# Rows loaded and normed a stage ahead, inverse roots on GpSimd, projections as paired row tiles

## What is computed

```python
h = tok(x)                                  # q,k,v; (gamma * (q k^T)) v; Wo; prelu
h = concatenate([h, txt], axis=1)           # 8 x 1056 x 64
h = h + L0_attn(layernorm(h), ...)          # 8 heads of 8, softmax(q k^T + bias[i-j]) v, proj + bias
h = h + L0_ffn(layernorm(h), ...)           # top 2 of 16 experts 64->128->64, then a layernorm
h = h + L1_attn(layernorm(h), ...)          # linear attention: elu+1, q (k^T v), Wproj + bias
h = h + L1_ffn(layernorm(h), ...)           # rmsnorm, 4 heads with rope, causal softmax, wo; rmsnorm, top 2 of 8 experts (silu)
```

## Time and profile before

| | |
|---|---|
| median of three runs | 2918.41 us (2917.83 to 2937.95) |
| profiled execution, its own time | 2931.52 us |
| its span | 2929.7 us |
| busy: PE, DVE, ACT, POOL | 88%, 68%, 53%, 12% |
| mean granted PE clock | 0.887 |

### The profile page before, as it was taken

One profiled execution on the slowest core, in us unless ns is written; L12 is line 12 of the kernel. 1 busy time (PEld: TensorE's weight loads), 2 busy tenths in 40 slices (PEclk: granted clock), 3 DMA queues, 4 the chain that ended last, 5 costly groups with the idle time before them and its releaser, 6 DMA issues. The chain is left out here.

```text
span 2929.7 us, 52672 instructions
## 1 busy us (share of the span) xinstructions
PE 2564.9 (88%) x18552; PEld 1160.8 (40%) x18552; DVE 1987.7 (68%) x5083; ACT 1552.4 (53%) x2645; POOL 354.0 (12%) x456
## 2 busy tenths in 40 slices
PE   5987659999999999997699997986679998789999
PEld 3323542333333333335333333564544444623333
DVE  5686668888888888871477775737667774256665
ACT  2332654777777777772244443615646666134443
POOL 1020100000000000003112211011101011221110
PEclk9998767999999999996699997755589999589999
DMA  2101991112212212213300001233422231511100
GB/s 72 22 15 27 279 281 51 48 45 55 56 38 56 55 38 55 70 17 85 67 17 17 22 16 24 61 85 124 160 104 72 66 91 35 123 28 29 29 15 20
DMA packets 308491, 188.23 MB, mean 64 GB/s; under 512 B 262069, under 2 KB 263414, under 8 KB 306982
## 3 DMA queue, kind: packets, MB, share of 16 engines
q1 hardware_dynamic: 297870, 165.80, 21.4%
q0 software_dynamic: 10368, 19.06, 2.1%
HBM read 103.16 MB, written 81.69 MB: 63 GB/s over the span
## 5 line engine op out<-in xcount | busy, mean ns | idle before, releaser
L1614 DVE TENSOR_REDUCE att_mpart<-ps 128x1 f32<-128x512 f32 x1024 | 637.3, 684 | 81.2 <-PE ps L1423 48.5
L1571 ACT ACTIVATE att_p<-ps 128x704 f32<-128x704 f32 x768 | 543.3, 760 | 139.5 <-PE ps L1487 134.5
L1516 PE MATMUL ps<-att_p,att_v 128*32 128x352 f32 x3072 | 308.4, 472 | 0.1
L1423 PE MATMUL ps<-att_kT,att_qT 64*128 64x512 bf16 x1024 | 274.5, 387 | 27.5 <-DMA att_qz<-qt_d 14.2
L1487 PE MATMUL ps<-att_qm,att_kT 64*128 64x352 bf16 x1536 | 251.1, 317 | 10.8 <-ACT att_p L1571 8.0
L1243 DVE TENSOR_REDUCE cau_mpart<-ps 128x1 f32<-128x512 f32 (+5 forms) x384 | 193.5, 552 | 90.8 <-PE ps L1069 70.7
L2285 ACT ACTIVATE mo_act<-ps,mo_b 128x768 f32<-128x768 f32 x176 | 156.3, 901 | 129.5 <-PE ps L2167 129.5
L2478 DVE TENSOR_TENSOR mo_g<-mo_act,ps 128x768 f32<-128x768 f32 x176 | 167.4, 951 | 79.5 <-PE ps L2202 43.5
L1210 ACT ACTIVATE cau_p<-ps 128x704 f32<-128x704 f32 (+6 forms) x272 | 171.6, 660 | 82.5 <-PE ps L1128 49.7
L2865 ACT ACTIVATE mo_act<-ps 128x1024 f32<-128x1024 f32 (+1 forms) x108 | 102.9, 953 | 196.3 <-PE ps L2779 196.0
L1487 PEld LDWEIGHTS ps<-att_qm,att_kT 64*128 64x128 bf16 x1536 | 82.4, 93 | 279.8 <-issue 263.6
(11 more groups left out here) (432 smaller groups left out, 4367.2 us busy)
## 6 DMA issues: line engine op xcount, KB each, us to landing
v_d<-pre_v SPq DMA_DIRECT2D x32, 288.0 KB, 4.3
qs_d<-pre_qs SPq DMA_DIRECT2D x8, 1152.0 KB, 5.6
att_qs<-qs_d SPq DMA_DIRECT2D x32, 288.0 KB, 4.5
att_v<-v_d SPq DMA_DIRECT2D x32, 288.0 KB, 4.4
qt_d<-pre_qT SPq DMA_DIRECT2D x8, 1056.0 KB, 4.4
kt_d<-pre_kT SPq DMA_DIRECT2D x8, 1056.0 KB, 7.6
att_kT<-kt_d SPq DMA_DIRECT2D x32, 264.0 KB, 2.7
att_qT<-qt_d SPq DMA_DIRECT2D x32, 264.0 KB, 3.1
```

Of the source, the lines that this page charges most:

```text
L1423: mm = pe.matmul(ps[:, bank, :], qT[half(s), u, j * P:(j + 1) * P], kT[half(s), u, c * BANK:(c + 1) * BANK], start=True, stop=not near)
L1516: mm = pe.matmul(ps[32 * cg:32 * cg + 32, 7, 0:TH], v[:, u, i, s, :], p[:, r, s, :], start=i < 2, stop=i == FULL - 1)
L1571: e = act.activation(p[:, n % PRING, :, :], ps[:, bank:bank + 2, 0:TH], ACT.Exp)
L1614: red = dve.tensor_reduce(mpart[:, j, s, c:c + 1], ps[:, bank, :], AX.X, ALU.max)
```

## The change

*First rows and norms a stage ahead.* The next stage's `fetch` now also loads its first rows (batches or steps 0 and 1; in the attentions, units 0 and 1). A new `early` lets DVE or POOL, at a given place of a stage, run a part of the next stage's first norm: the whole norm in `token_mix` at its last n == 10; the corner parts in `heads_prep`; statistics and, a batch later, scaling for `moe`, `measure` for `causal_prep` and `stats` for `expert_units` in the last two batches of a projection; zeroing, `measure` and `norm` of `linear_attn` in the last steps of `moe`, with its root on POOL. A projection calls `ahead` one batch sooner. PE may enter the stage behind `moe` when the last add is made.

*Roots.* `heads_prep` and `linear_attn` take the inverse root by `pow` on POOL. In `moe` step 0's root goes ahead of the casts.

*Projections.* Eight full tiles are turned as four pairs of 128 x 128; xT then has an even tile's 64 columns on partitions 0 to 63 and an odd tile's on 64 to 127. The products of a pair go to the two halves of the array's rows, into two PSUM banks. `front` has two PSUM buffers and is issued ahead of `turn`. The bias is added to the residual rows on POOL.

The core of the diff, each piece as it stands there:

```diff
     if who == "pe":
-        eng.wait_ge(done["act"], no)
-        eng.wait_ge(done["dve"], no)
+        left = const["psum_left"].get(no - 1)
+        if left is not None:
+            left(eng)
+        else:
+            eng.wait_ge(done["act"], no)
+            eng.wait_ge(done["dve"], no)
...
+def early(eng, const, who):
+    no = const["no"]
+    parts = const["early"].get((no + 1, who), [])
+    if parts:
+        if no > 0:
+            for x in ENGINES:
+                if x != who:
+                    eng.wait_ge(const["done"][x], no)
+        if no > 1:
+            eng.wait_ge(const["tidied"], no - 1)
+        parts.pop(0)(eng)
+def not_early(eng, const, who):
+    for part in const["early"].pop((const["no"], who), []):
+        part(eng)
...
+                    if last and n == 10:
+                        early(dve, const, "dve")
...
+            dve.wait_ge(rstd_made, b + 1)
+            at_least(dve, xt_mm, b * 3)
+            for t in range(NT):
+                dve.tensor_scalar(xn[:, t, :], h[:, par, t, :], stats[:, t, 0:1], rstd[:, t:t + 1], ALU.subtract,
+                                  ALU.mult).then_inc(xn_made, 1)
...
         def fetch(sp):
+            sp.wait_ge(tail_set, 1)
+            load(sp, 0, 0)
             sp.dma_start(w[0:C, :], a["L0_attn_qkv_w"]).then_inc(w_in, 16)
             sp.dma_start(w[C:C + 1, :], a["L0_attn_qkv_b"].rearrange("(o c) -> o c", o=1)).then_inc(w_in, 16)
             sp.dma_start(t126[:, :], a["L0_attn_rpb_table"][126:127, :].broadcast_to([P, H])).then_inc(t_in, 16)
+            load(sp, 1, 1)
+        const["early"][const["building"], "dve"] = [lambda dve: norm(dve, 0, 0)]
...
+            def root(b):
+                pool.wait_ge(var_made, b + 1)
+                pool.tensor_tensor(rstd[:, :], var[:, :], half[:, :], ALU.pow).then_inc(rstd_made, 1)
+                pool.wait_ge(rstd_made, b + 1)
+            root(0)
...
+                if b + 1 < B:
+                    root(b + 1)
...
-                if not last:
-                    root(b + 1)
...
+                if last:
+                    early(dve, const, "dve")
...
+        def fetch(sp):
+            for u in range(2):
+                load(sp, 0, u)
...
             sp.dma_start(craw[:, :, :], corner).then_inc(t_in, 16)
+            for u in range(2):
+                load(sp, 0, u)
+            sp.wait_ge(set_up, 2)
+            for u in range(2):
+                load_last(sp, 0, u)
...
+        def corner_parts(dve):
+            dve.memset(mrow[:, :, :], 0.0).then_inc(mrow_set, 1)
+            dve.wait_ge(t_in, 32)
+            dve.tensor_tensor(cdel[:, 0, :].rearrange("p (m h) -> p m h", h=8), craw[:, :, :],
...
+            for x in range(3):
+                dve.wait_ge(cor_rest, x + 1)
+                src = cdel[:, x, :].rearrange("p (m h) -> p h m", h=8)
...
+                if x < 2:
+                    dve.wait_ge(cor_hi, x + 1)
+                    dve.tensor_tensor(cdel[:, x + 1, :].rearrange("p (m h) -> p h m", h=8), src, cor[:, :, x, :],
...
+        const["early"][const["building"], "dve"] = [corner_parts]
...
+        FRONT, XT, Y = (0, 6), 2, 4
+        PAIRS = FULL // 2
...
+            for r in (0, C):
+                sp.dma_start(w[r:r + C, :], w_in_d).then_inc(S["w_in"], 16)
             if bias_d is not None:
-                sp.dma_start(w[C:KW, :], bias_d.rearrange("(o c) -> o c", o=1)).then_inc(S["w_in"], 16)
+                sp.dma_start(bias[:, :], bias_d.rearrange("(o c) -> o c", o=1).broadcast_to([P, C])).then_inc(S["w_in"], 16)
...
-                if b == B - 1:
+                if b == B - 2:
                     ahead(sp, const)
...
-            if bias_d is not None:
-                pool.memset(xT[C:KW, :, :], 1.0).then_inc(S["one_set"], 1)
-                pool.wait_ge(S["one_set"], 1)
...
+            def add_bias(b, par):
+                arrived(pool, res_in, b, par, 2)
+                pool.tensor_tensor(res[:, par, 0:FULL, :], res[:, par, 0:FULL, :], bias[:, :].unsqueeze(1)
+                                   .broadcast_to([P, FULL, C]), ALU.add).then_inc(S["b_made"], 1)
+                pool.wait_ge(S["b_made"], b * 2 + 1)
...
+                    .then_inc(S["b_made"], 1)
+                pool.wait_ge(S["b_made"], b * 2 + 2)
...
+                at_least(pe, S["xt_cp"], b * 2)
+                for m in range(PAIRS):
+                    if m in (0, PAIRS - 1):
+                        pe.wait_ge(S["att_made"], b * 3 + (1 if m == 0 else 2))
+                    mm = pe.transpose(ps[:, XT, m * P:(m + 1) * P], att[:, par, 2 * m:2 * m + 2, :].rearrange("p s c -> p (s c)"),
+                                      const["eye"][:, :])
+                mm.then_inc(S["xt_mm"], 1)
+                pe.wait_ge(S["att_made"], b * 3 + 3)
+                pe.transpose(ps[0:C, XT + 1, 0:TT], att[0:TT, par, FULL, :], const["eye"][0:TT, 0:TT]).then_inc(S["xt_mm"], 1)
...
                 at_least(pe, S["hn_made"], b * 2)
-                for t in range(NT):
-                    if t % 4 == 0:
-                        pe.wait_ge(S["xt_cp"], b * 3 + t // 4 + 1)
-                    bank, col = Y + t // FULL, t % FULL * C
-                    mm = pe.matmul(ps[0:rows(t), bank, col:col + C], xT[0:KW, par, t * P:t * P + rows(t)], w[0:KW, :],
-                                   start=True, stop=True)
-                    if t >= FULL - 1:
-                        mm.then_inc(S["y_mm"], 1)
-            pe.wait_ge(S["w_in"], 16 * (1 if bias_d is None else 2))
-            if bias_d is not None:
-                pe.wait_ge(S["one_set"], 1)
+                pe.wait_ge(S["xt_cp"], b * 2 + 1)
+                for m in range(PAIRS):
+                    for s in range(2):
+                        mm = pe.matmul(ps[:, Y + s, m * C:(m + 1) * C], xT[s * C:(s + 1) * C, par, m * P:(m + 1) * P],
+                                       w[s * C:(s + 1) * C, :], start=True, stop=True)
+                pe.wait_ge(S["xt_cp"], b * 2 + 2)
+                pe.matmul(ps[0:TT, Y, PAIRS * C:(PAIRS + 1) * C], xT[0:C, par, BANK:BANK + TT], w[0:C, :], start=True, stop=True)\
+                    .then_inc(S["y_mm"], 1)
...
-                turn(b, b % 2)
                 if b + 1 < B:
                     front(b + 1, (b + 1) % 2)
+                turn(b, b % 2)
...
+                act.wait_ge(S["xt_mm"], b * 2 + 1)
+                act.activation(xT[:, par, 0:BANK], ps[:, XT, :], ACT.Identity).then_inc(S["xt_cp"], 1)
+                act.wait_ge(S["xt_mm"], b * 2 + 2)
+                act.activation(xT[0:C, par, BANK:BANK + TT], ps[0:C, XT + 1, 0:TT], ACT.Identity).then_inc(S["xt_cp"], 1)
...
+                if b >= B - 2:
+                    early(dve, const, "dve")
...
         def fetch(sp):
+            load(sp, 0, 0)
             for r in (0, C):
...
+            load(sp, 1, 1)
...
+        def first_stats(dve):
+            for _, part in norm_parts[:-1]:
+                part(dve, 0, 0)
+        const["early"][const["building"], "dve"] = [first_stats, lambda dve: norm(dve, 0, 0)]
+        def left(pe):
+            pe.wait_ge(S["add_made"], MK)
+        const["psum_left"][const["building"]] = left
...
+                    if last and n == 4:
+                        early(pool, const, "pool")
...
             root(0, 0)
+            pool.wait_ge(S["rstd_made"], 1)
+            pool.wait_ge(S["gate_in"], 16 * 4)
+            for s in range(2):
+                pool.tensor_copy(sel[s * C:s * C + E3, :], sone[s * C:s * C + E3, :]).then_inc(S["sel_made"], 1)
+                pool.wait_ge(S["sel_made"], s + 1)
...
+                    if n == 0 and k == MK - 2 or n in (3, 8) and last:
+                        early(dve, const, "dve")
...
+        const["early"][const["building"], "dve"] = [lambda dve: stats(dve, 0)]
...
+        def root(pool, b):
+            pool.wait_ge(S["var_made"], b + 1)
+            pool.tensor_tensor(rstd[:, :], var[:, :], half[:, :], ALU.pow).then_inc(S["rstd_made"], 1)
+            pool.wait_ge(S["rstd_made"], b + 1)
+        def first_root(pool):
+            pool.memset(half[:, :], -0.5).then_inc(S["half_set"], 1)
+            pool.wait_ge(S["half_set"], 1)
+            root(pool, 0)
+        def zero_tail(dve):
+            dve.memset(h[:, :, FULL, :], 0.0).then_inc(S["zeroed"], 1)
         def fetch(sp):
+            sp.wait_ge(S["zeroed"], 1)
+            load(sp, 0, 0)
             sp.dma_start(wq[:, :], a["L1_attn_WqT"]).then_inc(S["w_in"], 16)
             sp.dma_start(wkv[:, :], a["L1_attn_WkvT"]).then_inc(S["w_in"], 16)
             sp.dma_start(block_of[:, :, :], a["block_of"]).then_inc(S["w_in"], 16)
+            load(sp, 1, 1)
+        const["early"][const["building"], "dve"] = [zero_tail, lambda dve: measure(dve, 0, 0), lambda dve: norm(dve, 0, 0)]
+        const["early"][const["building"], "pool"] = [first_root]
...
+        const["early"][const["building"], "dve"] = [lambda dve: measure(dve, 0, 0)]
```

549 lines of the change are left out of this document (259 added, 290 removed).

## The result

The changed kernel takes 2894.1 us, median of 5 runs (2892.5 to 2904.6), against 2922.0 of the kernel before (5 runs, 2917.8 to 2938.0): ratio 0.989, 95% interval 0.986 to 0.992. The forecast was 2848 us and a gain of 70; the measured gain is 28 between the medians. Between the two profiled executions it is 37.4 (2931.5 and 2894.1), all of it reached at PE's first product of the last stage (2568.07 and 2530.67), and the sum of 71.8 is held against that. The time lies inside the range, near its upper end.

What follows compares the result with a forecast made beforehand. It took 104 us of PE idle time at stage borders, plus the projections, as what could be gained. Terms summed to 71.8 us off the profiled 2931.5, or 2846.6 by the median; forecast 2848 us, range 2818 to 2900.

Steps and rivals of the forecast that it cites:

- the term of the linear attention: Linear attention: seven square-root table loads leave ACT, mostly hidden by PE at the lower clock; gain 2 us, bounds -6 and 12.
- Row tiles: Three projections: paired products run together in two array halves; 11.7 us in the second, 4 and 4.3 in first and third.
- Mixing to pre-attention: Batch 0's norm moves into token mixing: 6.6 us saved, 3.4 let come back as PE waits; net 3.2, bounds 0 and 7.
- Roots in pre-attention: Pre-attention, seven batches: ACT no longer waits for the variance, DVE waits for POOL's `pow`; gain 2.4 us.
- pre-attention to attention: Before attention, 14.20 us idle: early loads save, corner parts ahead of DVE's last copies cost 10.5; net 1.6, bounds -3 and 11.
- First projection to experts: Before the first experts, 19.35 us idle: 4.2 left for the gate's load, 5.7 lost to tail blocking; gain 9.4.
- one of my own signs of being wrong: The forecast is wrong if an idle time of over 10 us still stands before the expert stages.
- Experts to linear attention: PE waits only for the last add: 3.0 of 17.45 us idle left, 2.6 lost to inserted pieces; gain 11.8.
- The rival of the lower clock: Linear attention runs wholly at the lower clock, 20 to 40 us come back, 2880 us in all; chance 0.12.
- Slower than before: Pre-attention and linear attention: DVE waits for POOL's `pow`, POOL behind its casts; over 5.1 us a batch decides; chance 0.05.
- Second projection to causal preparation: Of 12.53 us idle, landing and statistics go, roots and scales stay, DVE's measuring blocks the tail; gain 6.8.
- Third projection: Faster products gain 4.3 us; the idle time before the second experts only moves, as POOL's square waits for norm weights, 0.5.

Runs made afterwards that it cites:

- the later pair of runs: Kernel with roots ahead of the store and early selection loads, with against without the early norm in token mixing: 2837.3 against 2839.0 us.

## Why the prediction was wrong

The largest step that failed is the term of the linear attention: forecast a gain of 2, measured a loss of 13.4. Next come the handover out of the first experts (11.8 forecast, 3.6 measured) and, smaller, the tail of the second projection, the norm inside mixing and the first experts' handover.

*What bounds the kernel.* Right: 104 us of idle time at the borders, and the change takes most of it away (63 of them).

*Row tiles.* Right. Head, loop and products were forecast at 1.9 + 2.5 + 11.7 + 4 + 4.3 = 24.4 us; alone the new projection brought 24.1. That it fits so well is luck in part: the second projection got 16.3 shorter, not 11.7, and 5.8 of that came back as idle time behind it, which the sum had not. The rule of the Trainium skill ("TensorEngine Tiling (Array Packing)", Key Properties) on draining at a switch of tiling mode, which spoke against it, would have kept a batch near 7.06 of PE. The rows show 4.56 without an idle time at the two switches, 0.2 above the forecast 4.35.

*Mixing to pre-attention.* Forecast a gain of 3.2, measured a later start by 1.9, and by the later pair of runs nothing. The step that failed is "I let 3.4 of it come back". All of it came back, 6.8 with DVE's 2.00 of waiting for `pow` in it. *Roots in pre-attention* and *pre-attention to attention*: 2.4 + 1.6 were forecast, and from the kernel before to the changed one the stage and the idle time behind it together got 2.4 shorter (154.4 to 152.0). Without the corner parts the stage takes 136.7 to 139.5 us against 138.8 to 140.2 with roots on ACT: the root's 2.4 is at best 1.5, the ranges overlap, and no run undoes it alone. The loads ahead alone took 2.6 to 2.7 off the idle time (14.2 to 11.5 or 11.6), and moving the corner parts cost about 2: I had the corner's 10.5 us on the path, but not the 2.76 for its table.

*First projection to experts.* 9.4 was forecast for the handover and the tail together. Idle fell by 7.4, with 12.0 left where I left 4.2, which was one of my own signs of being wrong. The selection table is issued at 1405.75, behind SP's last stores, and landing and cast follow. The tail's blocking I had at 5.7, and it is 5.86, so the term came to 1.5. With the head and the faster products the whole stage was forecast at 15.3 and brought 11.7.

*Experts to linear attention.* Forecast 11.8, measured 3.6: the idle time fell by 8.1, and the experts' stage got 4.5 longer. "PE waits only for the add" was wrong. PE waits at the head of the stage for the ones column of `va` as well, and its memset stands on POOL behind the experts' last work (1793.21, PE starts at 1793.68), so that 9.34 us stayed. With the memset a stage early it was 1.1.

*Linear attention.* This is the largest miss. Forecast a gain of 2 with bounds of -6 and 12; the stage lost 13.4, and 21 in the profiled executions of six kernels with the same code, outside of the bounds; its old code took 99.0 and 104.6 us in two. I costed what leaves ACT, the seven table loads, and gave no thought to where on POOL the root would stand: behind a store that waits for the output. Taking the table loads away is worth nothing (93.4 without them, 92.8 with them). So the upper bound of 31 us by the drain of the Trainium skill ("ScalarE: Activation LUTs", What ACT_TABLE_LOAD costs) is not seen either. Two rivals each had a part. The rival of the lower clock had the form of the loss, PE busy for longer at the lower clock, though its 20 to 40 us are more than the 13 to 21 measured and it had no cause for it; its chance was 0.12. "Slower than before" had the in-order queues, but looked for POOL behind its casts and not behind its store, and its 5.1 us a batch are far from the 1.9 measured (13.4 over seven batches).

*Second projection to causal preparation.* The sum with the row tiles was 18.5 beside the head, measured 13.1; what is missing is the tail's standstill of 11.24 us in the changed kernel. There DVE waits 10.04 us for rows that SP may load only behind POOL's memset, and it is then held for 1 us more by POOL's further memsets. *Into causal attention*: forecast 9.7, idle fell by 9.2. *Third projection*: 4.8 forecast, 4.3 measured, right by luck. Faster products and a shorter idle time paid for the 14.21 us that PE stood for the norm weights. I had named that wait and costed it at nothing beyond what it saves.

In one line: the idle time at the borders went and the row tiles' gain came about as forecast, and 34 of the 72 us are missing for two reasons. What is inserted into an in-order queue waits there for its own inputs (root behind store, norm behind landing, sum behind weights), and in the linear attention PE ran at the lower clock for longer. The sum is closed by some 6 us that no term had: the causal preparation was 3.9 shorter and the two attentions 1.0 each.

Open: why token mixing takes 255 to 258 us in some executions and 263 in others with the same code; and what exactly decides when PE's clock falls in the linear attention, where one order of the queue gave 93.4 us in one execution and 106.5 in another.

## What to carry to other kernels

Moving an operation ahead to hide its wait only helps if its inputs have landed by the place where it now stands in the engine's queue; otherwise the wait moves with it, and all that stands behind pays. Load first, two or three batches ahead, and only then insert the work (norm inside the projections' tails, by the stages: 9.6 us gained with early rows, 8.2 lost with late ones, of which only the first shows in the total). When a small operation is given to an idle engine, read that engine's queue and not its busy share: POOL was 12% busy, and the root behind one store went with a linear attention of 112 to 120 us, where the root ahead of it gave 93 to 106. And read the queue again after each move of a load: one of the moves here left it in the same place.

## What was not expected of the hardware

- A DVE instruction on 128 x 9 numbers took 4.13 us beside POOL memsets of 3.94 and 2.02, and 0.17 without them; one on 128 x 384 took 2.13 beside POOL's casts, and 0.56 without them.
- The same 456 passes of PE took 83.6, 93.0 and 105.9 us at mean granted clocks of 0.81, 0.72 and 0.62, and of the three the kernel with most idle time in the stage (9.8 us of 93.4) had the highest clock.
- Whole-array transposes and two row tiles in turn, twice a batch, leave no gap in PE's rows: 1.06, 0.26, 1.97 and 0.42 us back to back.
